# Two layers in one kernel: shared unit's last step behind the sorted steps, the last layer's gate product on GpSimd and its first tile begun in attention's last row

## The chip, the cores and the metric

One core of a Trainium2 chip runs the program, in one launch. The metric is the device time of one execution in microseconds, from the profile's start of the program to its end on that core. All times are medians of several executions where nothing else is said.

## What is computed

4096 tokens of 256 numbers (float32) go through two layers. Each has an attention part and a feed-forward part, both wrapped in the same way: layernorm, scale and shift from a conditioning vector, the part, a gate, and the addition to the tokens.

```python
h = _layernorm(x) * (1 + cb) + sb
x = x + gb * _L0_ffn_ref(h, ...)        # layer 0: two rounds of experts
h = _layernorm(x) * (1 + ca) + sa
x = x + ga * _L1_attn_ref(h, ...)       # layer 1: linear attention, 16 heads
h = _layernorm(x) * (1 + cb) + sb
x = x + gb * _L1_ffn_ref(h, ...)        # layer 1: 8 experts, top 2
```

The feed-forward part of layer 0 runs two rounds. In each, a token goes to 2 of 6 experts, chosen and weighted by a router, and also to 2 shared units, which see every token; their outputs and the token itself are added and normalised. The feed-forward part of layer 1 (stage D below) returns `x + experts(rms(x))`, with `x` being the modulated `h`: so the last layer's result is `x + gb*h + gb*experts(...)`. The term `gb*h` is "the gate product".

## The kernel before, in words

The instructions of each engine are written out by hand, engine by engine, with semaphores between them; an engine runs its own list in order. The stages are A (attention of layer 0), B (its two rounds of experts), C (attention of layer 1) and D (experts of layer 1). The tokens stay in SBUF as `b.x`, 8 tiles of 512 tokens (`NB = 8`), each of 4 chunks of 128.

**Stage B.** A round has 37 steps of 512 rows: 8 "new" (shared unit 0 on tile t), 8 "old" (shared unit 1 on tile t, whose product is joined to that of the new step, so that one down-projection does for both) and 21 "sort" steps (`NBB = 21`), each a block of 512 rows of one expert. `Round` (L1004) lists them. Every engine goes through iterations j = -1 to 36, and in iteration j it deals with up to three steps: `now` = j, `after` = j + 1, `third` = j + 2. TensorE (`b_tensor`, L1181) does:

```python
gate(after); turn(third); up(after); down(now)
```

where `turn` transposes the rows of a step. For a sort step it waits for the four indirect gathers that bring its rows (`r.gathered`). Weights are loaded raw by SyncE (`b_sync`, L1044, into four buffers `w_raw`), rounded by ScalarE and split into a low part by VectorE for each step that is `fresh`; shared units are so once a round. Between iterations 6 and 12 the routing goes on beside the steps; its last product is the index of the gathers, computed by VectorE in `index_vector` (L1698, L1704) at the end of iteration 12. GpSimd (`b_gpsimd`, L1709) then issues six blocks' gathers, and from then on four gathers and four scatters by turns; the gathers of the first four blocks wait for the transposes of the last old step, because all share the four buffers `got`, and scatters of a block wait for `r.o`, its output in `b.sent`, which VectorE writes in `send` (L1555). VectorE's order in an iteration is: low parts and transposed rows of `third`, product of `after` (for an old step also the addition of the shared product, L1539), output of `now`. When all scatters have landed, the next round, or stage C, fetches the rows back (`fetch_sync`, L1128; `close_sync`, L1779).

**Stage C** (`m_vector`, `m_tensor`, `m_scalar`, `m_gpsimd`) is a pipeline over the tiles; iterations j run from -3 to 9. At j = 8 VectorE divides tile 7 (`divide`) and adds the output of tile 6 to the tokens (`project`, L1988), at j = 9 that of tile 7. Each is there as soon as TensorE has it.

**Stage D's preparation** starts on every engine when the last tile is through (`rc.x`). Per tile: VectorE takes mean and variance (`stats`, L2116, L2120), GpSimd 1/sqrt (`rs`, L2168 and L2170, with a small op of the helper `absorb` at L178 ahead of it), VectorE modulates (`modulate`, two passes over four chunks, L2130 and L2134) into `p_h`, ScalarE sums squares, GpSimd takes 1/sqrt of that (`rs2`), TensorE transposes (L2231), ScalarE copies, TensorE multiplies by the router (L2236) and by a diagonal matrix of the gate (L2244, `p_diag`): that is the gate product, and VectorE adds it to the tokens from PSUM (`residual`, L2147). VectorE's order is modulate(t), stats(t+1), residual(t-1), logits(t-1). Behind tile 7's logits and residual the routing begins (`routed_vector`, L921).

## Time and profile before

| | us |
|---|---|
| three runs | 2035.42, 2036.41, 2038.35; median 2036.41 |
| the profiled execution | 2036.51 |
| its span, first to last instruction | 2034.6 |
| TensorE busy | 1766.5 (87%) |
| VectorE busy | 1402.5 (69%) |
| ScalarE busy | 1029.3 (51%) |
| GpSimd busy | 821.1 (40%) |
| mean granted TensorE clock | 0.927 of full speed |

A line of the timeline gives start and duration in us from the span's start, the engine (PE is TensorE, PEld its weight loads, DVE VectorE, ACT ScalarE, POOL GpSimd, SP SyncE), the line of the kernel, the operation, what it writes and reads, the shapes, how many were merged into the line, and in brackets how long the engine had been idle before and what released it. L167 is the line of a helper that makes every three-pass matmul of the experts. In busy times a DMA issued by GpSimd counts as its instruction. Shares of the whole span are averages over stages with different limits; the stretches that the change touches are read one by one below.

### The profile page before, as it was taken

The numbers are of one execution on the slowest core, as the hardware profiler recorded it, in microseconds if no ns is written. First come the engines' busy times: TensorE is split into PE (matmuls) and PEld (weight loads), VectorE is DVE, ScalarE is ACT, GpSimd is POOL, SyncE is SP. The second block draws the span as 40 slices with busy tenths as digits, with TensorE's granted clock in tenths as the row PEclk, the third lists the DMA queues.
The fourth block names the chain that finished last, engine by engine and source line by source line (L and its number), as shares of the span: only waits on it lengthen the run. The fifth ranks groups of instructions, "written<-read, shape, count | busy, mean of one in ns | idle before, by whom it ended". The sixth has DMA issues, their size and how long they took to land. (4 is left out here: it accounts for less than half of the span.)

```text
span 2034.6 us, 31786 instructions
## 1 busy us (share of the span) xinstructions
PE 1766.5 (87%) x11154; PEld 1559.6 (77%) x11154; DVE 1402.5 (69%) x2513; ACT 1029.3 (51%) x2078; POOL 821.1 (40%) x868
## 2 busy tenths in 40 slices
PE   5899999999978999999949999996499883899990
PEld 4788888888877878888838788886266683899990
DVE  4665556546433888777756987775798687688886
ACT  4344334434412344555546355553688353788882
POOL 2132232323211114777721157776221030788840
PEclk8899999999998899999969999998699966899995
DMA  4100000000023131666553226664600013688857
GB/s 155 62 1 11 10 10 0 10 10 0 10 88 103 55 105 40 202 192 202 168 190 122 91 78 199 203 186 146 221 32 1 1 63 114 206 278 277 257 193 258
DMA packets 146216, 231.43 MB, mean 114 GB/s; under 512 B 28082, under 2 KB 103092, under 8 KB 141108
## 3 DMA queue, kind: packets, MB, share of 16 engines
q1 hardware_dynamic: 122484, 165.47, 24.6%
q0 software_dynamic: 23616, 64.52, 10.5%
q8 instruction: 60, 0.98, 0.2%
q14 instruction: 56, 0.46, 0.1%
HBM read 174.07 MB, written 55.33 MB: 113 GB/s over the span
## 5 line engine op out<-in xcount | busy, mean ns | idle before, releaser
L178 POOL TENSOR_TENSOR spare_g<-neg_half 128x1 f32<-128x1 f32 x80 | 20.7, 259 | 622.2 <-ACT a_sg L538 142.5
L167 PE MATMUL bank<-gT_hi,w_hi 128*128 128x512 f32 x592 | 246.0, 416 | 2.4 <-DVE gT_lo L1526 2.4
L167 PE MATMUL bank<-gT_hi,w_lo 128*128 128x512 f32 x592 | 237.3, 401 | 0.0
L167 PE MATMUL bank<-gT_lo,w_hi 128*128 128x512 f32 x592 | 236.2, 399 | 0.0
L1731 POOL DMA_INDIRECT got<-b_rows,b_gather_i x168 | 171.9, 1023 | 65.1 <-issue 50.6
L1526 DVE TENSOR_TENSOR gT_lo<-bank,gT_hi 128x512 fp32r<-128x512 f32 x148 | 97.0, 689 | 132.4 <-ACT gT_hi L1334 99.1
L1364 ACT ACTIVATE m_hi<-gs 128x512 fp32r<-128x512 f32 x116 | 73.0, 633 | 128.3 <-DVE gs L1533 69.0
L167 PEld LDWEIGHTS bank<-gT_hi,w_lo 128*128 128x128 f32 x592 | 113.2, 191 | 27.6
L167 PE MATMUL bank<-w_hi,m_hi 128*128 128x256 f32 x464 | 130.5, 281 | 2.8 <-DVE shared L1555 1.4
L167 PEld LDWEIGHTS bank<-gT_hi,w_hi 128*128 128x128 f32 x592 | 113.6, 192 | 22.9 <-DVE gT_lo L1526 2.5
L167 PEld LDWEIGHTS bank<-gT_lo,w_hi 128*128 128x128 f32 x592 | 113.9, 192 | 21.5
L167 PE MATMUL bank<-w_lo,m_hi 128*128 128x256 f32 x464 | 130.4, 281 | 0.0
L167 PE MATMUL bank<-w_hi,m_lo 128*128 128x256 f32 x464 | 130.1, 280 | 0.0
L2390 POOL DMA_INDIRECT d_got<-d_rows,d_gather_i x78 | 95.7, 1227 | 68.8 <-DVE d_gather_i L2321 45.4
L2396 POOL DMA_INDIRECT d_kept<-d_sent,d_scatter_i x78 | 97.6, 1252 | 45.9 <-DVE d_sent L2551 24.6
L884 POOL TENSOR_TENSOR a_aTm<-a_aT,masks 128x512 f32<-128x512 f32 x56 | 71.4, 1286 | 107.2 <-PE bank L416 82.6
L1355 ACT ACTIVATE gs<-bank,w_cols 128x512 f32<-128x512 f32 x84 | 57.7, 690 | 97.3 <-PE bank L167 97.3
L1738 POOL DMA_INDIRECT b_kept<-sent,b_scatter_i x88 | 90.4, 1028 | 26.8 <-issue 26.8
L167 PE MATMUL bank<-d_gT_hi,v_hi 128*128 128x256 f32 x312 | 93.0, 298 | 1.8 <-DVE d_gT_lo L2531 1.8
L577 ACT ACTIVATE a_ax<-bank 128x512 f32<-128x512 f32 x48 | 28.7, 597 | 128.0 <-PE bank L416 128.0
L1334 ACT ACTIVATE gT_hi<-bank 128x512 fp32r<-128x512 f32 x148 | 82.0, 598 | 21.1 <-PE bank L1202 20.9
L167 PE MATMUL bank<-v_hi,d_m_hi 128*128 128x256 f32 x312 | 91.3, 293 | 1.4 <-issue 0.9
(455 smaller groups left out, 5731.2 us busy)
## 6 DMA issues: line engine op xcount, KB each, us to landing
v_raw<-in_units SPq DMA_DIRECT2D x39, 1024.0 KB, 5.0
w_raw<-in_units SPq DMA_DIRECT2D x52, 256.0 KB, 4.9
shared<-in_units SPq DMA_DIRECT2D x40, 256.0 KB, 4.4
b_rows<-x SPq DMA_DIRECT2D x16, 512.0 KB, 2.9
got<-b_rows SPq DMA_DIRECT2D x16, 512.0 KB, 3.9
close_back<-b_kept SPq DMA_DIRECT2D x16, 512.0 KB, 7.8
d_back<-d_kept SPq DMA_DIRECT2D x16, 512.0 KB, 8.5
w_raw<-b_folded SPq DMA_DIRECT2D x24, 256.0 KB
```

The source lines that it names most:

```text
L167: ins = pe.matmul(out, a, b, start=first and n == 0, stop=last and n == of - 1)
L178: eng.tensor_tensor(b.spare_g[:, i:i + 1], b.neg_half[:, 0:1], b.neg_half[:, 0:1], ALU.mult)
L577: act.activation(b.ax[:, :], B[1][:, :], ACT.Copy).then_inc(s.ax.sem, 1)
L884: g.tensor_tensor(four(b.aTm[l % 2][:, :]), four(b.aT[:, :]), mid(b.maskT[:, l, :], CT), ALU.mult).then_inc((s.aTm if l else s.aTm0).sem, 1)
L1334: act.activation(b.gT_hi[st.par][:, f, :], B[6 + f][:, :], ACT.Copy).then_inc(r.gT_hi.sem, 1)
L1355: act.activation(product_of(b, st)[:, o, :], B[2 + o][:, :], ACT.Silu, bias=b_bias(b, st, 1, o)).then_inc(r.sg.sem, 1)
L1364: act.activation(b.m_hi[st.par][:, o, :], b.gs[:, o, :], ACT.Copy).then_inc(r.m_hi.sem, 1)
L1526: v.tensor_tensor(b.gT_lo[st.par][:, f, :], B[6 + f][:, :], f32(b.gT_hi[st.par][:, f, :]), ALU.subtract).then_inc(r.gT_lo.sem, 1)
L1731: g.indirect_dma_start(b.got[:, kg % 4, c, :], None, dram.rows[rnd], bass.IndirectOffsetOnAxis(b.gather_i[:, q:q + 1], 0)).then_inc(r.gath ...
L1738: g.indirect_dma_start(dram.kept[rnd], bass.IndirectOffsetOnAxis(b.scatter_i[:, q:q + 1], 0), b.sent[kg % SENDS][:, c, :], None).then_inc( ...
L2390: g.indirect_dma_start(b.got[n % 6][:, c, :], None, rows, bass.IndirectOffsetOnAxis(b.gather_i[:, q:q + 1], 0)).then_inc(r.gathered[n % 6] ...
L2396: g.indirect_dma_start(kept, bass.IndirectOffsetOnAxis(b.scatter_i[:, q:q + 1], 0), b.sent[k % 4][:, c, :], None).then_inc(r.scattered[k % ...
```

## The change

Three things:

1. In stage B the old step of tile 7 goes behind the 21 sort steps (`LATE = 1`). Its unit's weights are loaded, rounded and split again (`LATE_LOAD`), its rows reloaded into a buffer of `got` that has come free; the gathers of the first blocks wait for the old step that is last now (tile 6). The order of the buffers of the next stage's fetches is turned, so that the late step's buffers are taken last, and two waits are put into SyncE's queue: before the third fetch of round 1, and before the constants of stage C. Stage C's buffers move within SBUF.
2. In stage C, at j = 8, VectorE does D's statistics of tiles 0 and 1 and D's modulation of tile 0. The waits for `rc.x` at the start of D fall away on VectorE, ScalarE and GpSimd, and on TensorE it stands behind the transposes of tile 0.
3. In D's preparation GpSimd multiplies the modulated tile by the gate, in two halves of 128x512 per tile, into a new buffer `p_gh`; the first half stands before 1/sqrt of the next tile, the second behind it. The 16 diagonal matmuls per tile and the two products that made the diagonal are gone. VectorE's residual is one addition of 128x1024 from SBUF.

```diff
+C_GAP = 5168
...
-STEPS, LB, WM = 2 * NB + NBB, 2 + NBB, KD * D
+LATE = 1
+FRONT_STEPS, LATE_LOAD = 2 * NB - LATE, 2 + NBB
+STEPS, LB, WM = 2 * NB + NBB, 3 + NBB, KD * D
...
-        order = [("new", t) for t in range(NB)] + [("old", t) for t in range(NB)] + [("sort", k) for k in range(NBB)]
+        order = [("new", t) for t in range(NB)] + [("old", t) for t in range(NB - LATE)]
+        order += [("sort", k) for k in range(NBB)] + [("old", t) for t in range(NB - LATE, NB)]
...
-            load = {"new": 0, "old": 1}.get(kind, 2 + n)
+            load = {"new": 0, "old": 1 if j < FRONT_STEPS else LATE_LOAD}.get(kind, 2 + n)
...
+
+
+def row_slot(t, rnd):
+
+    return t % 4 if t < NB - LATE else (rnd * NBB + NBB + t - (NB - LATE)) % 4
...
-    q0, t0, expert = rnd * LB, rnd * NB, {0: slice(0, 1), 1: slice(1, 2)}
+    q0, t0, expert = rnd * LB, rnd * NB, {0: slice(0, 1), 1: slice(1, 2), LATE_LOAD: slice(1, 2)}
...
-            sp.wait_ge(r.joined.sem, r.joined.at(rnd * NB + NB - 1))
-        if n >= 2:
+            sp.wait_ge(r.joined.sem, r.joined.at(rnd * NB + NB - LATE - 1))
+        if 2 <= n < LATE_LOAD:
...
         for t in range(BACKS):
+            if t == BACKS - 1:
+                sp.wait_ge(r.gT_ps.sem, r.gT_ps.at(STEPS - 1))
             fetch_sync(sp, b, r, dram.kept[0], t)
...
-    for t in range(NB):
+    for t in range(NB - LATE):
...
-            biases(n - 1)
+            if n - 1 < LATE_LOAD:
+                biases(n - 1)
+    for t in range(NB - LATE, NB):
+        sp.wait_ge(r.gT_ps.sem, r.gT_ps.at(first_sort(rnd * NBB + NBB - 4 + t - (NB - LATE))))
+        sp.dma_start(b.got[:, row_slot(t, rnd), :, :], rows_of(dram.rows[rnd], t)).then_inc(r.reloaded[t % 4].sem, 16)
...
-    return (kg // NBB) * STEPS + 2 * NB + kg % NBB
+    return (kg // NBB) * STEPS + FRONT_STEPS + kg % NBB
...
-    return (kg // NBB) * OUTS + NB + kg % NBB
+    return (kg // NBB) * OUTS + NB - LATE + kg % NBB
...
-            src = lambda c, f: b.got[:, t % 4, c, f * P:(f + 1) * P]
+            src = lambda c, f: b.got[:, row_slot(t, rnd), c, f * P:(f + 1) * P]
...
-    first, rounds = 2 * NB, (NBB - 2) // TURNS
+    first, rounds = FRONT_STEPS, (NBB - 2) // TURNS
...
-            act.wait_ge(done.sem, done.at(rnd * (OUTS if done is r.down_ps else STEPS) - 1))
+            ended = LATE if st.load % LB == 0 else 0
+            act.wait_ge(done.sem, done.at(rnd * (OUTS if done is r.down_ps else STEPS) - 1 - ended))
...
         if k >= 4:
...
         else:
-            g.wait_ge(r.gT_ps.sem, r.gT_ps.at(rnd * STEPS + 2 * NB - 1))
+            g.wait_ge(r.gT_ps.sem, r.gT_ps.at(rnd * STEPS + FRONT_STEPS - 1))
...
     old_rows(0)
+    sp.wait_ge(r.o.sem, r.o.at(2 * OUTS - 1))
     sp.dma_start(b.heads, d["consts"][:, 1, :]).then_inc(s.load_c_small.sem, 16)
...
+        if j == NB:
+            d_stats_vector(v, after, q, 0)
         if is_tile(j - 1):
             divide(j - 1)
+        if j == NB:
+            d_modulate_vector(v, after, q, 0)
         if is_tile(j - 2):
             project(j - 2)
+        if j == NB:
+            d_stats_vector(v, after, q, 1)
         if is_tile(j):
...
         if is_tile(j + FRONT - 2):
...
-    def stats(t):
...
-    def modulate(t):
...
+def d_stats_vector(v, b, r, t):
...
+def d_modulate_vector(v, b, r, t):
...
+        v.wait_ge(r.gh.sem, r.gh.at(t - 2))
...
-        for i in range(2):
-            v.wait_ge(r.gh.sem, r.gh.at(t, i + 1))
-            xt = b.x[:, (t * CT + 2 * i) * D:(t * CT + 2 * i + 2) * D]
-            v.tensor_tensor(xt, xt, b.bank[6 + i][:, :], ALU.add).then_inc(r.xh.sem, 1)
-
-    stats(0)
-    for k in range(KD):
-        v.tensor_tensor(b.p_diag[:, k, :], b.ident, b.mod[:, GB, k * P:(k + 1) * P], ALU.mult).then_inc(r.diag.sem, 1)
-    for t in range(NB):
-        modulate(t)
+        v.wait_ge(r.gh.sem, r.gh.at(t))
+        v.tensor_tensor(tile_of(b, t), tile_of(b, t), flat(b.p_gh[t % 2][:, :, :]), ALU.add).then_inc(r.xh.sem, 1)
+
+    for t in range(1, NB):
+        d_modulate_vector(v, b, r, t)
...
-            stats(t + 1)
-        if t >= 1:
-            residual(t - 1)
-            logits(t - 1)
+            d_stats_vector(v, b, r, t + 1)
+        residual(t - 1)
+        logits(t - 1)
...
+    def gated(t, i):
+        par = t % 2
+        g.wait_ge(r.h.sem, r.h.at(t, 2 * i + 2))
+        if t >= 2:
+            g.wait_ge(r.xh.sem, r.xh.at(t - 2))
+        g.tensor_tensor(b.p_gh[par][:, 2 * i:2 * i + 2, :], b.p_h[par][:, 2 * i:2 * i + 2, :], mid(b.mod[:, GB, :], 2), ALU.mult).then_inc(r.gh.sem, 1)
+
     rs(0)
     for t in range(NB):
+        gated(t, 0)
         if t + 1 < NB:
             rs(t + 1)
+        gated(t, 1)
         rs2(t)
...
         pe.wait_ge(r.hT.sem, r.hT.at(t))
+        if t == 0:
+            pe.wait_ge(m.x.sem, m.x.at(NB - 1))
...
-        if t >= 1:
-            pe.wait_ge(r.xh.sem, r.xh.at(t - 1))
-        for c in range(CT):
-            for k in range(KD):
-                at = (c % 2) * D + k * P
-                ins = pe.matmul(b.bank[6 + c // 2][:, at:at + P], b.p_hT[par][:, k, c * P:(c + 1) * P], b.p_diag[:, k, :], start=True, stop=True)
-            if c % 2:
-                ins.then_inc(r.gh.sem, 1)
...
-                b.back = [b.got[:, 2 * i:2 * i + 2, :, :] for i in range(2)] + [b.sent_both]
+                b.back = [b.sent_both, b.got[:, 2:4, :, :], b.got[:, 0:2, :, :]]
...
-            b.close_back, b.x_old = [sb(sc, f"close_back{t}", [P, PICKS, CT, D]) for t in range(CLOSE_BUFS)], [sb(sc, f"x_old{t}", [P, CT, D]) for t in range(CLOSE_BUFS)]
...
+            b.x_old = [sb(sc, f"x_old{t}", [P, CT, D]) for t in range(1, CLOSE_BUFS)]
+            b.c_gap = sb(sc, "c_gap", [P, C_GAP])
+            b.x_old.insert(0, sb(sc, "x_old0", [P, CT, D]))
+            b.close_back = [sb(sc, f"close_back{t}", [P, PICKS, CT, D]) for t in range(CLOSE_BUFS)]
...
-                b.p_h, b.p_xn, b.p_sq = ([sb(e, f"pd_{n}{i}", [P, CT, D]) for i in range(2)] for n in ("h", "xn", "sq"))
+                b.p_h, b.p_gh, b.p_xn, b.p_sq = ([sb(e, f"pd_{n}{i}", [P, CT, D]) for i in range(2)] for n in ("h", "gh", "xn", "sq"))
...
-                b.p_diag = sb(e, "pd_diag", [P, KD, P])
...
-            m_vector(v, bC, s, link, rb, rp, rc)
+            m_vector(v, bC, s, link, rb, rp, rc, bD, rd)
...
-                       rs2=("wu_lo", 1), hn=("weighed", CT), gh=("mixed", 2), xh=("added", 2), hT_ps=("hT", KD), hT=("folded", KD), logit_ps=("logit_ps", 1), logits=("logits", 1),
+                       rs2=("wu_lo", 1), hn=("weighed", CT), gh=("mixed", 2), xh=("added", 1), hT_ps=("hT", KD), hT=("folded", KD), logit_ps=("logit_ps", 1), logits=("logits", 1),
...
-        rd.router, rd.diag = signal("d_router", KD), signal("d_diag", KD)
...
-            g.wait_ge(rc.x.sem, rc.x.at(last))
...
-            act.wait_ge(rc.x.sem, rc.x.at(last))
...
-            pe.wait_ge(rc.x.sem, rc.x.at(last))
-            d_prep_tensor(pe, bD, rd)
+            d_prep_tensor(pe, bD, rd, rc)
...
```

## Rows read from the trace of the kernel before

**Rows 1.** The page: its first line.
```profile
span 2034.6 us, 31786 instructions
```

**Rows 2.** Instruction groups of GpSimd, 804 to 1029: busy us, mean ns | idle before.
```profile
L1731 POOL DMA_INDIRECT got<-b_rows,b_gather_i x84 | 86.5, 1030 | 32.6 <-issue 25.3 <-PE bank L1202 7.3
```

**Rows 3.** Timeline of GpSimd: start us, us, instruction [idle before <-releaser].
```profile
804.70 1.22 POOL L1731 DMA_INDIRECT got<-b_rows,b_gather_i  x1 [7.30 <-PE bank L1202]
...
1023.60 0.97 POOL L1738 DMA_INDIRECT b_kept<-sent,b_scatter_i  x1 [0.30 <-issue]
...
1413.06 0.97 POOL L1738 DMA_INDIRECT b_kept<-sent,b_scatter_i  x1 [0.30 <-issue]
```

**Rows 4.** Timeline of VectorE in the token steps.
```profile
803.25 0.20 DVE L1704 TENSOR_SCALAR b_gather_i<-b_gather_i 128x84 int32<-128x84 int32 x1
...
1014.71 1.28 DVE L1555 TENSOR_TENSOR shared<-bank,w_b 128x512 f32<-128x512 f32 x2
...
1019.26 0.69 DVE L1555 TENSOR_TENSOR sent<-bank,w_b 128x512 f32<-128x512 f32 x1 [0.66 <-PE bank L167]
...
1409.99 0.69 DVE L1555 TENSOR_TENSOR sent<-bank,w_b 128x512 f32<-128x512 f32 x1 [0.66 <-PE bank L167]
```

**Rows 5.** Timeline of VectorE, last layer's preparation.
```profile
1622.66 0.69 DVE L1988 TENSOR_TENSOR x<-x,bank 128x512 f32<-128x512 f32 x1 [1.27 <-PE bank L2058]
...
1633.67 1.67 DVE L2130 SCALAR_TENSOR_TENSOR pd_h<-x,p_mv,mod 128x256 f32<-128x256 f32 x4 [1.66 <-POOL p_rs L2170]
...
1638.58 0.68 DVE L2147 TENSOR_TENSOR x<-x,bank 128x512 f32<-128x512 f32 x1
...
1677.11 1.66 DVE L2130 SCALAR_TENSOR_TENSOR pd_h<-x,p_mv,mod 128x256 f32<-128x256 f32 x4
...
1689.54 0.28 DVE L921 COPY r_z<-logits 128x256 f32<-128x256 f32 x1
```

**Rows 6.** Instruction groups of VectorE, 1633.6 to 1677, columns as in rows 2.
```profile
L2147 DVE TENSOR_TENSOR x<-x,bank 128x512 f32<-128x512 f32 x12 | 8.1, 678 | 5.8 <-PE bank L2244 5.8
```

**Rows 7.** Timeline of TensorE in round 0.
```profile
802.71 1.09 PE L1202 MATMUL bank<-ident,got 128*128 128x128 f32 x8
...
812.56 1.04 PE L1202 MATMUL bank<-ident,got 128*128 128x128 f32 x8
...
999.67 1.03 PE L1202 MATMUL bank<-ident,got 128*128 128x128 f32 x8
```

**Rows 8.** Line 1731 by itself, its last line.
```profile
DMA to landing us min/median/max: 2.7/3.3/6.8
```

**Rows 9.** Timeline of TensorE after a long stop.
```profile
1734.55 1.97 PE L2434 MATMUL bank<-ident,d_got 128*128 128x128 f32 x8 [8.60 <-DMA d_got<-d_rows,d_gather_i]
```

**Rows 10.** Stretches, line 167: us, busy (count) of TensorE, weight loads, clock, DMA.
```profile
1734.00:1741.00 7.00, 3.50 (x16) 3.50 (x17) 0.50 0.38 97
```

**Rows 11.** Timeline of GpSimd in four places.
```profile
52.11 1.27 POOL L884 TENSOR_TENSOR a_aTm<-a_aT,masks 128x512 f32<-128x512 f32 x1 [3.99 <-PE bank L416]
...
1067.83 1.16 POOL L178 TENSOR_TENSOR spare_g<-neg_half 128x1 f32<-128x1 f32 x1 [10.90 <-ACT got L1428]
...
1439.23 1.13 POOL L1900 TENSOR_TENSOR p_rs<-p_rs,neg_half 128x4 f32<-128x4 f32 x1
...
1632.63 1.01 POOL L2170 TENSOR_TENSOR p_rs<-p_rs,neg_half 128x4 f32<-128x4 f32 x1
```

**Rows 12.** Timeline of VectorE in three of these places.
```profile
52.08 1.58 DVE L670 SCALAR_TENSOR_TENSOR a_h_next<-a_h_next,a_rs,mod 128x256 f32<-128x256 f32 x1
...
1067.71 1.23 DVE L1437 TENSOR_TENSOR x<-x,got 128x1024 f32<-128x1024 f32 x1
...
1438.25 1.64 DVE L1435 SCALAR_TENSOR_TENSOR close_back<-close_back,r_gb 128x256 f32<-128x256 f32 x4
```

**Rows 13.** Timeline of TensorE, first tile of the preparation.
```profile
1630.43 1.94 PE L2231 MATMUL bank<-ident,pd_h 128*128 128x128 f32 x8 [7.80 <-DVE pd_h L2134]
1633.06 3.58 PE L2236 MATMUL bank<-router_D,pd_hT 128*128 128x8 f32 x16 [0.69 <-ACT pd_hT L2200]
```

44 lines of the change are left out of this document (21 added, 23 removed).

## The prediction, made blind

> **What bounds the kernel now.** The edits touch three stretches, so I read the chain of waits first (in both rounds it runs through GpSimd's issues), then one timeline for each engine of each stretch. The execution read took 2036.51 us around a span of 2034.6 [rows 1]; the median of three runs is 2036.41, the same for this purpose. What can be told from no change is about 0.2%, or 4.1 us.
>
> *Token steps, both rounds.* The reader is to see that GpSimd, not TensorE, ends a round. In round 0 its 84 gathers and 84 scatters (44 and 40, by their two kinds of source) run from 804.70 to 1028.4; the only wait for another engine is the 7.3 us before the first gather, all else is issue gaps of 0.30 [rows 2]. VectorE has the last block's rows ready at 1019.95 (1019.26 + 0.69), but GpSimd starts their scatters only at 1023.60: 3.65 us of queue. In round 1 it is 1410.68 against 1413.06, 2.4 us [rows 3, 4]. The next stage starts from the last scatter.
>
> *Preparation of the last layer.* From the last residual of attention (1622.66 + 0.69 = 1623.35) to the start of routing (1689.54) go 66 us; from one tile's modulation to the next it takes (1677.11 - 1633.67)/6 = 7.24 us, of which VectorE waits about 1 us per tile for TensorE's gate product (5.8 us in six tiles) [rows 5, 6].
>
> **Edit 1: last shared-unit step moved behind the 21 sorted steps.** TensorE's order inside an iteration is gate(next), transposes(next but one), up(next), down(now). The first sorted block's transposes now stand where the last "old" step's stood: at 802.71 instead of 812.56 [rows 7]. They need four gathers. Those no longer wait for the old step's transposes (done 803.80, first gather 0.9 later) but for the index, finished at 803.45 [rows 3, 4, 7]. So the first gather starts at about 804.35, only 0.35 earlier. The fourth starts 3 x 1.33 (1.03 and the gap of 0.30 [rows 2]) = 4.0 later and lands 3.0 after that (the gathers of this line land 2.7 us after issue at the least, 3.3 in the median [rows 8]): 811.35. **TensorE stands for 8.7 us**, and the first block starts 1.2 us earlier than before instead of 9.85.
>
> Then the clock. After a stop of 8.60 us, TensorE comes back at 1734.55, and the granted clock is 0.50 (1.2 GHz, the lower of its two levels) up to 1741.0, 6.5 us on [rows 9, 10]. Half of 6.5 us is 3.2; TensorE has a little less than that to lose, as part of such a stretch is issue, and I take 3.0. Bounds: half of it (1.5) to half as much again (4.5).
>
> At the other end the sorted block is now followed by an old step. A sorted step takes (999.67 - 812.56)/20 = 9.36 us [rows 7]. Before, the last block's rows came 3.96 us after the last but one's (1019.95 - 1015.99 [rows 4]), as nothing stood in between. Now they come like those of a block in the middle, a full 9.36 after, and 1.3 later still, because VectorE adds the old step's shared product first (two more 128x512 passes, which cost what the two of the row at 1014.71 cost). Sum for round 0: -1.2 + 3.0 + (9.36 + 1.3 - 3.96) = +8.5, so the rows are ready at 1028.45, and the scatter starts 0.9 later: 1029.35 against 1023.60, **+5.75**. Round 1 has the same pattern with 1.25 us less queue: **+7.0**. GpSimd now waits for VectorE in front of the last four scatters in each round.
>
> The rest of edit 1 costs nothing as long as its cover stands. The shared unit is loaded again (768 KB) and rounded again: ScalarE and VectorE do for it what they do for every sorted block, in a place where before the last sorted block stood. On SyncE's queue its loads come after the biases of the last block but two, and the reload of the tile's rows comes last of all; SyncE has a whole step for it before TensorE wants it, and if that cover went, the late step alone would be later, and the last scatter with it since down(now) stands behind gate and up of the late step. The late step's own output ends some 5 us after the last block's, while scatters are issued and land. Two waits are added on SyncE's queue. Behind the one before the third fetch stand the stores and fetches of round 1, behind the one before the small constants stand attention's seven constant loads and the fetches of tiles 1 to 7; both end with the late step, while the first two fetches (or the three loads of tile 0) are still under way. The new order of buffers moves no work.
>
> **Edit 2: first tile begun in attention's last row of work.** VectorE's statistics of tile 0 fall into its idle time before the last division, its modulation before the last-but-one residual, statistics of tile 1 before the last one. VectorE waits there for TensorE anyway and the last residual keeps its 1623.35. Modulation of tile 1 begins then, against 1633.67 before [rows 5]: **-10.3**. The two diagonal products (0.5) are in it.
>
> **Edit 3: gate product by GpSimd.** Removed: 16 matmuls per tile and the wait for them. Added: two products of 128x512 on GpSimd per tile, priced by its nearest row, 1.27 us for the same shape with two SBUF inputs and one of them repeated [rows 11]. GpSimd's total per tile is 2.5 + 3.0 = 5.6 us, so it does not become the bound by its work. But the two engines get in each other's way:
> - At 52.08 VectorE starts a 128x256 op with two SBUF inputs 0.03 before GpSimd's product starts, and takes 1.58 us. Ops of this size take 0.40 to 0.48 undisturbed (four of them 1.64, at 1438.25), so **+1.10**: it stands until GpSimd is through [rows 11, 12]. Both halves of the new product meet such ops: the first is released by chunk 2 of the modulated tile, while VectorE writes chunk 3 and 4; the second is queued behind 1/sqrt of the next tile, which is just what VectorE's next modulation waits for. Two such stops per tile: 2.2.
> - The other way round, GpSimd's small op at 1067.83 takes 1.16 us instead of 0.19, to the end of VectorE's 128x1024 addition of two SBUF tiles that began at 1067.71 [rows 11, 12]. The residual becomes exactly this form (before, one input came from PSUM), and it starts right when GpSimd is to compute the next 1/sqrt. So its 1.22 lies in front of the 1.5 of that (VectorE's next modulation starts at 1633.67, 1.5 to 1.7 after its statistics end, the row of 1632.63 being its last part [rows 11]).
>
> Per tile: modulation and statistics 4.91 (1633.67 to 1638.58) + stops 2.2 + residual 1.22 + 1/sqrt 1.5 = **9.8 us in place of 7.24**. First interval 8.7 (no second half queued yet), five more of 9.8: tile 7 begins at 1623.35 + 8.7 + 49.0 = 1681.05, 3.9 later than 1677.11. Behind it: modulation 3.2 with two stops 2.1, transposes to logits at the low clock 6.2 (1630.43 to 1636.64 [rows 13]), logits and residual 1.5: 1694.1 against 1689.54, **+4.6** for edits 2 and 3 together. Bounds: +2.2 with the high clock at the end; +8.2 if a product takes 1.5.
>
> A rule weighed. While GpSimd computes 1/sqrt of four columns for 1.13 us at 1439.23, VectorE's four ops with two SBUF inputs, begun at 1438.25, go on at their usual pace (1.64) [rows 11, 12]; I give these small ops no price. The Trainium skill, page "SBUF — State Buffer", section "Who interferes with whom", has it that whichever of the two starts first holds the pair for its whole instruction and the other blocks fully. By that rule the second 1/sqrt of each tile would stop VectorE too; what it would give is a rival below.
>
> **Sum.** 2036.5 + 5.75 + 7.0 + 4.6 = 2053.85, say **2054**, 0.9% slower.
>
> **Rivals.**
> 1. *The product runs beside VectorE for nothing.* Place: the two stops and the late 1/sqrt per tile. Then a tile takes 4.91 + 1.5 + 0.1 = 6.5, tile 7 begins at 1662.4 and routing at 1673.3 (3.2 + 6.2 + 1.5 behind it): -16.2 in place of +4.6, so 2033, faster than before by 3; with the high clock at the end 2031. It decides where the tile falls under 7.24 + 10.3/6 = 8.9 us: below, the preparation gains. For it: GpSimd's work has room. Against it: [rows 11, 12], both ways. Chance 0.09.
> 2. *The late step costs nothing at the scatters* (GpSimd's queue still hides the last block; no stop of 8.7 us, or one that is made up). Then 2036.5 - 0.7 + 4.6 = 2040.4. For it: GpSimd has 2.4 to 3.65 us of queue. Against it: TensorE has no idle time between sorted steps to make anything up in. Chance 0.06.
> 3. *Both*: 2036.5 - 0.7 - 16.2 = 2019.6. Chance 0.04.
> 4. *Every GpSimd op stops VectorE*, the second 1/sqrt of each of seven tiles as well, 1.0 each: 2061. Against it: the last pair of [rows 11, 12]. This is the rule of the Trainium skill's page "SBUF — State Buffer" taken to the letter. Chance 0.05.
> 5. The forecast, 0.76.
>
> **Numbers.** The forecast's own range: edit 1 9.5 to 15.5 (clock 1.5 to 4.5 per round), edits 2 and 3 +2.2 to +8.2, not all at one end: 2047 to 2061. Down to rival 2 and up over rival 4: **2040 to 2062**, which leaves out rivals 1 and 3 and a little more. Faster by over 0.2% (under 2032.3): rival 3 and half of rival 1, 0.08. Within 0.2%: the rest of rival 1 and half of rival 2, 0.08. Slower: 0.84.
>
> **What would show it.** Right: in each round TensorE idle some 8 us before the first sorted block's transposes, released by a gather, then matmuls at half clock; GpSimd waiting for VectorE's output before the last four scatters; that scatter some 6 us later relative to the round's start; the new product at about 1.3 us, modulation ops of 1.5 us among those of 0.48, the small op in front of 1/sqrt at about 1.2 us, tiles 9.8 us apart. Wrong: tiles 6.5 us apart (edit 3), or the last scatter still preceded by an issue gap of 0.30 alone (edit 1).

## The result and the profile after

The changed kernel takes 2047.39 us (median of six executions, 2045.98 to 2053.41), the kernel before in the same session 2037.87 (2035.42 to 2044.20). The ratio is 1.0048, with a 95% interval from 1.0031 to 1.0065: slower by 0.5%, some 9.8 us. The prediction said slower, by 17.5 us. The signs and places were right; nearly every term was too large.

To see where the time went I cut both traces at the same marks. "Round" is from its first transposes to the start of the last block's four scatters, "seam" from there to the next round's first transposes, "attention" from the second round's mark to the end of the last residual, "preparation" from there to the start of routing.

| stretch | before | after | difference | forecast |
|---|---|---|---|---|
| start to first transposes of the token steps | 658.04 | 660.43 | +2.39 | 0 |
| round 0 | 365.56 | 369.00 | +3.44 | +5.75 |
| seam | 21.42 | 22.17 | +0.75 | 0 |
| round 1 | 368.04 | 371.04 | +3.00 | +7.0 |
| attention | 210.29 | 209.88 | -0.41 | 0 |
| preparation | 66.19 | 69.41 | +3.22 | +4.6 |
| rest of the last layer | 345.07 | 345.50 | +0.43 | 0 |
| span | 2034.61 | 2047.43 | +12.82 | +17.35 |

The first row is not the change's: among the 14 profiled kernels of this study, with the same work up to there, that mark stands at 657.9 to 658.6 in seven and at 659.9 to 660.5 in the other seven, kernels with and without the late step on either side; the kernel before happened to be among the early ones. What is left, 10.4, is close to the ratio.

The page's first line, against [rows 1]:

```profile
span 2047.4 us, 31578 instructions
```

**The token steps.** Instruction groups of GpSimd from 805 to 1035 us (columns as in [rows 2]):

```profile
L1747 POOL DMA_INDIRECT got<-b_rows,b_gather_i x84 | 85.3, 1015 | 31.6 <-issue 25.3 <-DVE b_gather_i L1720 6.3
L1754 POOL DMA_INDIRECT b_kept<-sent,b_scatter_i x44 | 45.0, 1024 | 17.9 <-issue 13.1 <-DVE sent L1571 4.8
```

The gathers now wait for the index and no longer for TensorE, and before the scatters there is a wait for VectorE's output that did not exist. The timeline of GpSimd puts it in front of the last block, in both rounds (against [rows 3]):

```profile
806.13 1.56 POOL L1747 DMA_INDIRECT got<-b_rows,b_gather_i  x1 [6.35 <-DVE b_gather_i L1720]
...
1029.43 0.97 POOL L1754 DMA_INDIRECT b_kept<-sent,b_scatter_i  x1 [4.84 <-DVE sent L1571]
...
1422.64 0.96 POOL L1754 DMA_INDIRECT b_kept<-sent,b_scatter_i  x1 [4.51 <-DVE sent L1571]
```

The timeline of VectorE shows what GpSimd waits for, the output of the last sorted block, in one line for its two halves (against [rows 4]); and the late step's own output, 4.8 us later, for which the trace shows nobody waiting:

```profile
1027.87 1.28 DVE L1571 TENSOR_TENSOR sent<-bank,w_b 128x512 f32<-128x512 f32 x2
1032.70 0.69 DVE L1569 TENSOR_TENSOR x<-x,bank 128x512 f32<-128x512 f32 x1 [3.55 <-PE bank L1261]
```

The timeline of TensorE (against [rows 7]): transposes of the old step in front, of the first, second and last sorted block and of the late step. The stop of 8.33 names no releaser; the first block's fourth gather starts at 810.49, so it is by this time, 2.8 us, that I take it for the landing. Between the first two sorted blocks stand 11.7 us, not 9.8 as before, and the matmuls inside begin 0.43 us apart up to 817.2 and 0.23 after it.

```profile
793.74 1.09 PE L1217 MATMUL bank<-ident,got 128*128 128x128 f32 x8 [0.16 <-DVE b_found L1710]
...
813.31 1.94 PE L1217 MATMUL bank<-ident,got 128*128 128x128 f32 x8 [8.33 <-issue]
...
825.01 1.04 PE L1217 MATMUL bank<-ident,got 128*128 128x128 f32 x8
...
1002.32 0.93 PE L1217 MATMUL bank<-ident,got 128*128 128x128 f32 x7
...
1011.63 0.60 PE L1217 MATMUL bank<-ident,got 128*128 128x128 f32 x4
```

Two stretches behind that stop (columns as in [rows 10], here all lines: us, busy of TensorE, weight loads, VectorE, ScalarE, GpSimd, granted clock, DMA):

```profile
813.00:815.00 2.00, 1.69 (x9) 1.72 (x9) 0.00 (x0) 0.57 (x1) 1.69 (x2) 0.50 0.41 109
815.00:820.00 5.00, 5.00 (x24) 4.21 (x23) 3.55 (x6) 1.14 (x3) 3.78 (x5) 0.76 0.31 90
```

**The preparation.** Timeline of VectorE and GpSimd, end of the last residual and one whole tile (against [rows 5, 11]):

```profile
1631.83 0.69 DVE L2005 TENSOR_TENSOR x<-x,bank 128x512 f32<-128x512 f32 x1 [1.27 <-PE bank L2081]
1632.43 1.67 DVE L2154 SCALAR_TENSOR_TENSOR pd_h<-x,p_mv,mod 128x256 f32<-128x256 f32 x4
...
1650.44 1.26 POOL L2206 TENSOR_TENSOR pd_gh<-pd_h,mod 128x512 f32<-128x512 f32 x1
...
1650.61 2.57 DVE L2154 SCALAR_TENSOR_TENSOR pd_h<-x,p_mv,mod 128x256 f32<-128x256 f32 x4 [1.43 <-POOL p_rs L2189]
...
1652.52 1.12 POOL L2199 TENSOR_TENSOR p_rs<-p_rs,neg_half 128x4 f32<-128x4 f32 x1
...
1653.10 2.67 DVE L2157 SCALAR_TENSOR_TENSOR pd_h<-pd_h,p_rs,mod 128x256 f32<-128x256 f32 x4
...
1654.05 1.44 POOL L2206 TENSOR_TENSOR pd_gh<-pd_h,mod 128x512 f32<-128x512 f32 x1 [0.40 <-DVE pd_h L2157]
...
1657.42 1.19 DVE L2170 TENSOR_TENSOR x<-x,pd_gh 128x1024 f32<-128x1024 f32 x1
...
1657.58 1.08 POOL L181 TENSOR_TENSOR spare_g<-neg_half 128x1 f32<-128x1 f32 x1 [2.09 <-DVE p_mv L2142]
...
1659.01 1.01 POOL L2189 TENSOR_TENSOR p_rs<-p_rs,neg_half 128x4 f32<-128x4 f32 x1
```

Each pass of four takes 2.6 us beside a product in place of 1.67 alone: two stops per tile. Ahead of the first pass VectorE waits 1.43 us. The second 1/sqrt (1652.52) lies beside both passes, and the sum of 2.57 + 2.67 has room for the two stops and nothing else: it stops nobody. From 1632.43 one interval of 8.64 and five of 9.54 lead to tile 7 at 1688.76; routing begins at 1701.93.

### The profile page after: what moved, and what is told of

It is laid out like the page before. It is cut to its first block and busy times, and to the rows that moved or that the text cites. A ratio compares the mean times of both kernels' runs of the same rounds, so it can differ in the third digit from the quotient of the medians.

```text
span 2047.4 us, 31578 instructions
## 1 busy us (share of the span) xinstructions
PE 1759.2 (86%) x11026; PEld 1552.0 (76%) x11026; DVE 1418.9 (69%) x2509; ACT 1031.0 (50%) x2084; POOL 850.4 (42%) x884
## 3 DMA queue, kind: packets, MB, share of 16 engines
q0 software_dynamic: 23616, 64.52, 10.3%
## 5 line engine op out<-in xcount | busy, mean ns | idle before, releaser
L181 POOL TENSOR_TENSOR spare_g<-neg_half 128x1 f32<-128x1 f32 x80 | 27.0, 338 | 591.3 <-ACT a_sg L541 142.3
L1380 ACT ACTIVATE m_hi<-gs 128x512 fp32r<-128x512 f32 x116 | 72.9, 633 | 128.9 <-DVE gs L1549 67.5
L170 PEld LDWEIGHTS bank<-w_hi,m_hi 128*128 128x128 f32 x464 | 88.0, 190 | 8.0 <-issue 5.5
L1754 POOL DMA_INDIRECT b_kept<-shared,b_scatter_i x80 | 82.8, 1035 | 25.3 <-issue 24.1
```

The lines of the kernel that those rows point to most:

```text
L170: ins = pe.matmul(out, a, b, start=first and n == 0, stop=last and n == of - 1)
L181: eng.tensor_tensor(b.spare_g[:, i:i + 1], b.neg_half[:, 0:1], b.neg_half[:, 0:1], ALU.mult)
L1380: act.activation(b.m_hi[st.par][:, o, :], b.gs[:, o, :], ACT.Copy).then_inc(r.m_hi.sem, 1)
L1754: g.indirect_dma_start(dram.kept[rnd], bass.IndirectOffsetOnAxis(b.scatter_i[:, q:q + 1], 0), b.sent[kg % SENDS][:, c, :], None).then_inc( ...
```

## The experiments

All kernels were timed against the kernel before on the same chip and in the same session, where its median was 2037.9 to 2042.1; the expectations count from the 2036.4 that stand above, so the ratio is what to compare. The stretches are those of the table above; "steps" is round 0, seam and round 1 together.

| kernel | ratio [95%] | steps | attention | preparation | rest |
|---|---|---|---|---|---|
| before | 1 | 755.02 | 210.3 | 66.19 | 345.1 |
| changed | 1.0048 [1.0031, 1.0065] | 762.20 | 209.9 | 69.41 | 345.5 |
| late_only | 1.0037 [1.0024, 1.0050] | 761.83 | 209.4 | 67.54 | 346.6 |
| prep_only | 1.0007 [0.9999, 1.0016] | 754.86 | 213.7 | 69.47 | 345.0 |
| first_only | 0.9921 [0.9908, 0.9934] | 754.78 | 209.8 | 52.69 | 344.9 |
| late_down_first | 1.0011 [1.0002, 1.0021] | 754.20 | 213.3 | 67.75 | 346.4 |
| late_early_index | 0.9988 [0.9978, 0.9999] | 749.53 | 212.3 | 67.71 | 346.5 |
| late_both | 0.9969 [0.9959, 0.9979] | 745.75 | 212.4 | 68.34 | 346.0 |
| prep_no_product | 0.9950 [0.9935, 0.9965] | 755.15 | 210.1 | 56.98 | 345.7 |
| prep_resid_first | 1.0017 [1.0008, 1.0026] | 754.49 | 209.9 | 70.92 | 345.8 |
| prep_rs_between | 0.9933 [0.9916, 0.9950] | 754.50 | 209.9 | 56.07 | 344.8 |
| combo | 0.9904 [0.9887, 0.9920] | 742.67 | 211.5 | 53.99 | 346.8 |
| combo_tuned | 0.9895 [0.9878, 0.9911] | 745.26 | 212.3 | 53.27 | 345.6 |
| after_repaired | 0.9890 [0.9869, 0.9912] | 744.86 | 212.8 | 56.06 | 344.6 |

Attention's length is one thing to know before reading on: 209.4 to 213.7 us, without order in the edits (prep_only and prep_rs_between have the same token steps and the same attention, and differ by 3.8). A single profile is therefore good for a stretch, not for a total; totals are compared by the ratios.

**late_only: edit 1 by itself.** The functions of the last layer and of attention are those of before; against the changed kernel:

```diff
-            m_vector(v, bC, s, link, rb, rp, rc, bD, rd)
+            m_vector(v, bC, s, link, rb, rp, rc)
...
-            d_prep_tensor(pe, bD, rd, rc)
+            pe.wait_ge(rc.x.sem, rc.x.at(last))
+            d_prep_tensor(pe, bD, rd)
...
```

> Edit 1 alone (with its buffers and the two waits on SyncE's queue), the last layer's preparation as before. By the steps of the prediction, with the sizes that the two traces show (the row of sorted blocks begins 1.6 us earlier against the step in front of it, the low clock costs 1.9, the last rows come 6.55 later behind their block, 3.4 us of GpSimd's queue are used up): +3.5 in round 0, about +4 in round 1, so +7.5: 2044. Rival: the changed kernel is also 2.4 us late before its token steps begin; if the moved buffers or the added waits do that, this kernel shows it too and stands at +10, 2046.5. Rival: the late step costs nothing at the scatters, 2036.

Measured 1.0037, some 7.6 us, as the first theory had it; with prep_only's 1.0007 it makes 1.0044, inside the changed kernel's interval. Its rounds are the changed kernel's (369.0 and 371.4). In its profile the token steps are 6.8 longer than before; the preparation and the rest are 1.3 and 1.6 longer too, with the same work (see the last section), so the agreement of 7.6 with 7.5 is partly chance. Its seam is 21.44, as before: the 0.75 of the changed kernel's seam is left without a cause.

**prep_only: edits 2 and 3 by themselves.** The moved buffers and the two added waits of edit 1 stay in.

```diff
-LATE = 1
+LATE = 0
-STEPS, LB, WM = 2 * NB + NBB, 3 + NBB, KD * D
+STEPS, LB, WM = 2 * NB + NBB, 2 + LATE + NBB, KD * D
```

> Edits 2 and 3 alone (the late step is off, LATE = 0). By the steps with measured sizes: tile 1 is modulated 10.3 us earlier, six tiles take 9.5 instead of 7.24, and the tail 1 to 2 more: +3.4, so 2040. The product counts with two stops of VectorE of 1.0 each per tile, the late small op with 1.0. Rival: edits 2 and 3 lengthen the rest of the last layer as well (routing starts 12.5 later in the changed kernel, the end is 12.8 later), +5 or more.

The preparation takes 69.47, the 3.3 more that were expected; the rest of the layer is unchanged, so the rival falls. The ratio's upper end, 1.0016, is just these 3.3 us; by the ratio alone this kernel can't be told from the kernel before. Its rounds are those of before (365.5 and 367.9), so the moved buffers and the added waits cost nothing there.

**first_only: edit 2 by itself.** In d_prep_vector, d_prep_gpsimd and d_prep_tensor the gate product is the diagonal one of before.

```diff
-        gated(t, 0)
         if t + 1 < NB:
             rs(t + 1)
-        gated(t, 1)
```

> Edit 2 alone: the first tile is begun in attention's last row, the gate product stays with TensorE and its diagonal. If the early start is worth what the prediction gave it, tile 1 is modulated at the end of the last residual (plus 0.5 for the diagonal) and the tiles stay 7.24 apart: -9.5, so 2027. Rival: TensorE, which cannot start tile 0's transposes before attention's last product, becomes the bound for the first tiles and takes the gain back: -3 to -5, 2032. Rival: nothing gained, 2036.

All three theories were too cautious: 0.9921, 16 us faster, and the preparation is 13.5 shorter. From the last residual's end to tile 1 it is 0.3 (1625.04 to 1625.36) in place of 10.3, as expected; but the tiles also stand only 6.75 apart, not 7.24. Timeline of this kernel, VectorE and TensorE:

```profile
1643.76 1.28 DVE L2171 TENSOR_TENSOR x<-x,bank 128x512 f32<-128x512 f32 x2
...
1645.60 1.67 DVE L2153 SCALAR_TENSOR_TENSOR pd_h<-x,p_mv,mod 128x256 f32<-128x256 f32 x4 [0.46 <-POOL p_rs L2192]
...
1652.02 1.95 PE L2259 MATMUL bank<-router_D,pd_hT 128*128 128x8 f32 x16 [1.38 <-ACT pd_hT L2222]
```

The two residual additions are one line without a wait between them, where before the second waited 1 us per tile for the product [rows 6]. With tile 0 begun early, TensorE's product of a tile is there when VectorE comes to it; the loop is VectorE's own work and 0.46 of waiting. Measured from this kernel, edit 3 costs 69.4 - 52.7 = 16.7 us, not the few that stand between the changed kernel and the kernel before. Of these, 1.3 lie behind tile 7, where TensorE's clock differs as well. Stretches from tile 7 to routing, changed kernel and first_only (columns as above):

```profile
1688.76:1701.93 13.17, 7.91 (x36) 7.32 (x35) 7.63 (x12) 6.08 (x18) 7.86 (x9) 0.50 0.25 87
...
1665.84:1677.73 11.89, 10.18 (x72) 9.75 (x72) 6.21 (x14) 6.25 (x19) 2.99 (x6) 0.86 0.36 122
```

The granted clock is 0.50 (1.2 GHz) there in all six kernels without the gate product on TensorE, prep_no_product among them, and 0.70 to 0.86 in the eight that have it; in the kernel before it is 0.86. The clock is not what the 1.3 us are, though: prep_no_product (below), at 0.50 and without the two stops of 1.9, takes 11.3 for this stretch, so what the lower clock costs there, the missing matmuls save.

**late_down_first: the end of a round.** In the iteration of the last sorted block, on TensorE and on VectorE:

```diff
+        ahead_of_late = j == FRONT_STEPS + NBB - 1
+        if ahead_of_late:
+            down(now)
         if after is not None:
             gate(after)
...
-        if now is not None and now.out is not None:
+        if now is not None and now.out is not None and not ahead_of_late:
             down(now)
...
+        ahead_of_late = j == FRONT_STEPS + NBB - 1
+        if ahead_of_late:
+            send(now)
         if after is not None:
             gated(after)
...
```

> Edit 1 alone, but in the iteration in which the last sorted block is finished, TensorE does its down-projection ahead of the late step's gate and up, and VectorE writes its output ahead of the late step's product. If the loss at the end of a round is the 9.36 + 1.3 - 3.96 us by which the last block's rows come later (measured 6.55), they come 4 us after the block before again, GpSimd's own queue hides them, and the last scatter starts about 1 us earlier than in the kernel before (with the first gather): -3.5 to -4.5 per round against the late step alone, so 2035 to 2037. Rival: the end of a round hangs on the late step's own output or on its reload: no change against the late step alone, 2044.

Measured 1.0011: 5.3 us of late_only's 7.6 are gone (7 to 9 were expected). In the profile the token steps are 7.6 shorter than late_only's and 0.8 shorter than before; what keeps the ratio above 1 lies behind them (preparation and rest are 1.6 and 1.3 longer than before, last section). Timeline of this kernel, end of round 0 (SPq is SyncE's DMA queue):

```profile
1022.58 0.69 DVE L1574 TENSOR_TENSOR sent<-bank,w_b 128x512 f32<-128x512 f32 x1 [0.65 <-PE bank L170]
...
1024.72 0.97 POOL L1760 DMA_INDIRECT b_kept<-sent,b_scatter_i  x1 [0.30 <-issue]
...
1031.52 0.68 DVE L1529 TENSOR_TENSOR w_lo<-w_raw,w_hi 128x512 fp32r<-128x512 f32 x1
1032.23 0.33 SPq L1077 DMA_DIRECT2D w_raw<-in_units  x1
1032.74 0.93 SPq L1147 DMA_DIRECT2D sent<-b_kept  x2
```

In front of the last scatters there is again nothing but the issue gap, and round 0 takes 364.5, 4.5 less than with the late step alone and 1.1 less than before. But the seam grows from 21.4 to 23.8. The fetches (1032.74) stand on SyncE's queue behind a load of the next round's weights, which waits for VectorE's low part of the late step (that is one of two limits here; combo_tuned below takes it away, and the seam stays as long). So the cover that the prediction gave to the late step's extra work holds only as long as the last scatters are late themselves.

**late_early_index: the start of a round.**

```diff
-ROUTE_AT, COUNT_AT, INVERT_AT, GATES_AT = NB - 2, NB - 1, NB + 1, NB + 5
+ROUTE_AT, COUNT_AT, INVERT_AT, GATES_AT = NB - 2, NB - 1, NB, NB + 5
...
         if j == COUNT_AT + 1:
             places_vector(v, b, link, r)
+            hot_vector(v, b, r, rnd, 0)
...
-        if j == COUNT_AT + 1:
-            hot_vector(v, b, r, rnd, 0)
```

ScalarE's first quarter of the same work goes behind the weights of its iteration.

> Edit 1 alone, with the routing's inversion begun one iteration earlier (iterations 8 to 11 instead of 9 to 12), so that the index of the gathers is ready about 11 us before TensorE reaches the first sorted block. Its first quarter must be built inside iteration 8, where VectorE takes 3.8 us more ahead of the product and TensorE waits for it: some 4 to 5 us lost there. If TensorE's 8 us without rows and the low clock behind them (1.9 by the sorted blocks' own interval) are what spoils the late step's start, they are gone: 10 gained, 4 to 5 lost, -5 to -6 per round against the late step alone, 2033 to 2036. Rival: gathers that start 11 us earlier only move the wait (GpSimd, at 1.3 us per issue, or the reload), and nothing is gained: 2045 or more.

Measured 0.9988, 10 us less than late_only, 5 per round (6.1 and 6.3 by the profiles). Timelines of this kernel, GpSimd's first gather and TensorE's first sorted block:

```profile
799.21 1.22 POOL L1748 DMA_INDIRECT got<-b_rows,b_gather_i  x1 [7.77 <-PE bank L1217]
...
807.07 0.49 PE L1217 MATMUL bank<-ident,got 128*128 128x128 f32 x3
```

The gathers wait for the old step's transposes again, and TensorE comes to the first block without a stop, 9.8 us behind the transposes of the step in front (797.28) instead of 19.6. The 20 intervals of the sorted blocks are back at 187.1 us, as before, where late_only has 189.0 and 188.7: the 1.9 and 1.6 were the stop's. The price stands before it: from the first step's transposes to the fifteenth's it is 138.9 us, 5.6 more than before. 9.8 + 1.9 - 5.6 is the 6.1 of round 0. The last scatters still wait for VectorE (4.49 us at 1021.28).

**late_both: start and end.** Both diffs together.

> Edit 1 with the earlier index and with the last sorted block's down-projection ahead of the late step's gate. If the two losses add, it stands at -5 to -6 per round for the start and, as GpSimd's queue runs ahead now and no longer hides anything, up to -5 per round for the end: 2023 to 2030. What can take it back: SyncE's queue, where the fetches of the next stage stand behind the next round's first weights, which wait for VectorE's low part of the late step (seen in the kernel with the down-projection first: fetches 1.8 us later than the landing of the scatters allows).

Measured 0.9969, which is 2030 from the 2036.4 of the first runs: the upper end of the range. Round 0 takes 360.0 (5.5 less than before), round 1 361.7 (6.3 less), and the seam 24.05 takes 2.6 back. With these two moves the late step gains: edit 1 was not wrong in itself. Neither move was tried without the late step; there the gathers wait for the last old step, and the index is ready 0.35 us earlier than that (803.45 against 803.80 [rows 4, 7]), so I would expect little of the first.

**prep_no_product: what the two products cost.** This kernel leaves the gate out, so it computes another result; it is prep_only with the two products shrunk to 128x1 and one more wait.

```diff
+        v.wait_ge(r.xh.sem, r.xh.at(t - 2))
...
-        v.tensor_tensor(tile_of(b, t), tile_of(b, t), flat(b.p_gh[t % 2][:, :, :]), ALU.add).then_inc(r.xh.sem, 1)
+        v.tensor_tensor(tile_of(b, t), tile_of(b, t), flat(b.p_h[t % 2][:, :, :]), ALU.add).then_inc(r.xh.sem, 1)
...
-        g.tensor_tensor(b.p_gh[par][:, 2 * i:2 * i + 2, :], b.p_h[par][:, 2 * i:2 * i + 2, :], mid(b.mod[:, GB, :], 2), ALU.mult).then_inc(r.gh.sem, 1)
+        g.tensor_tensor(b.p_gh[par][:, 2 * i, 0:1], b.p_h[par][:, 2 * i, 0:1], b.mod[:, GB, 0:1], ALU.mult).then_inc(r.gh.sem, 1)
```

> Edits 2 and 3 alone, with GpSimd's two products of 128x512 per tile shrunk to 128x1 (this leaves out the gate: the residual adds the ungated tile). Everything else stays. If the two products cost what VectorE's two stops of 1.0 and 1.1 show, a tile takes 7.5 instead of 9.54 us: modulation and statistics 4.9, small op held back by the residual 1.1, 1/sqrt 1.4; the preparation is 14 shorter, 2027. Rival: the interval is set by the chain residual, small op, 1/sqrt alone and stays above 9.

Tiles 7.63 apart (tile 2 to tile 7: 1631.17 to 1669.33), so the two products cost 9.54 - 7.63 = 1.91 per tile, which is the two stops. The ratio is 0.9950 where prep_only has 1.0007, the preparation 12.5 us shorter (14 were expected). Timeline of this kernel, VectorE and GpSimd:

```profile
1658.97 1.19 DVE L2171 TENSOR_TENSOR x<-x,pd_h 128x1024 f32<-128x1024 f32 x1
...
1659.13 1.08 POOL L181 TENSOR_TENSOR spare_g<-neg_half 128x1 f32<-128x1 f32 x1 [2.16 <-DVE p_mv L2142]
...
1661.69 1.67 DVE L2155 SCALAR_TENSOR_TENSOR pd_h<-x,p_mv,mod 128x256 f32<-128x256 f32 x4 [1.43 <-POOL p_rs L2190]
```

Both passes are back at 1.67; the held small op and the 1.43 of waiting are still there.

**prep_resid_first: the small op set free.**

```diff
         d_modulate_vector(v, b, r, t)
+        residual(t - 1)
         if t + 1 < NB:
             d_stats_vector(v, b, r, t + 1)
-        residual(t - 1)
         logits(t - 1)
```

> Edits 2 and 3 alone, with the residual ahead of the next tile's statistics instead of behind them. GpSimd's small op in front of 1/sqrt then meets no addition of two SBUF inputs. If it is the residual that holds it back (1.08 instead of 0.19 in each tile), the interval falls by 0.9 to 8.65 and the preparation by 5 to 6: 2035. Rival: the small op is late for another reason (it waits for the statistics in any case), no change: 2041.

The small op does take 0.19 now, and it is of no use: 1.0017, tiles 9.79 apart, 0.25 more than with the hold-back. The same view of this kernel:

```profile
1669.29 0.19 POOL L181 TENSOR_TENSOR spare_g<-neg_half 128x1 f32<-128x1 f32 x1 [3.23 <-DVE p_mv L2142]
...
1669.83 1.01 POOL L2189 TENSOR_TENSOR p_rs<-p_rs,neg_half 128x4 f32<-128x4 f32 x1
...
1670.97 2.58 DVE L2154 SCALAR_TENSOR_TENSOR pd_h<-x,p_mv,mod 128x256 f32<-128x256 f32 x4 [1.68 <-POOL p_rs L2189]
```

VectorE pays the residual's 1.2 us in either place, and then waits for all of 1/sqrt (1.68). My expectation took the delay of an engine's op for a cost of the loop without asking what the other engine does in that time.

**prep_rs_between: 1/sqrt hidden.** In d_modulate_vector:

```diff
-    v.wait_ge(r.rs.sem, r.rs.at(t))
+    v.wait_ge(r.mv.sem, r.mv.at(t))
...
+    v.wait_ge(r.rs.sem, r.rs.at(t))
     for c in range(CT):
         v.wait_ge(r.xn.sem, r.xn.at(t, c + 1))
```

> Edits 2 and 3 alone, with VectorE's wait for 1/sqrt between the two passes of the modulation. If small op and 1/sqrt behind the residual (1.4 us of VectorE's waiting per tile) are the other half of edit 3's price, the first pass hides them: a tile takes 8.1 us (9.54 - 1.43), with the two stops still there, and the whole 8 to 9 less than edits 2 and 3 alone. Rival: GpSimd's queue (both products, two 1/sqrt, small ops, 5.6 us and more where they are held back by the first pass) moves behind and its second product or 1/sqrt becomes what VectorE waits for: 9 us per tile, 3 less.

Better than either theory: tiles 7.30 apart, the preparation 56.07, ratio 0.9933. With GpSimd's product in place, edits 2 and 3 now gain 14 us against before. The same view of this kernel:

```profile
1648.34 1.39 DVE L2138 BATCH_NORM_STATS2 p_stats<-x 128x6 f32<-128x256 f32 x4
...
1648.86 1.27 POOL L2207 TENSOR_TENSOR pd_gh<-pd_h,mod 128x512 f32<-128x512 f32 x1
...
1651.27 1.66 DVE L2154 SCALAR_TENSOR_TENSOR pd_h<-x,p_mv,mod 128x256 f32<-128x256 f32 x4
...
1651.88 1.13 POOL L2190 TENSOR_TENSOR p_rs<-p_rs,neg_half 128x4 f32<-128x4 f32 x1
1652.98 1.26 POOL L2207 TENSOR_TENSOR pd_gh<-pd_h,mod 128x512 f32<-128x512 f32 x1
...
1653.05 2.67 DVE L2158 SCALAR_TENSOR_TENSOR pd_h<-pd_h,p_rs,mod 128x256 f32<-128x256 f32 x4
```

Two things went away: the wait of 1.43 (the first pass starts right behind the logits, and 1/sqrt lies beside it), and one of the two stops, which was not the aim. GpSimd's order has shifted by half a tile, so one of its products falls under VectorE's statistics, whose four ops take 1.39 as ever. 1.43 + 0.9 is the 2.24 by which the tile is shorter, nearly. Against first_only, which leaves the product on TensorE, the preparation is still 3.4 us longer: edit 3 is made cheap, not made to pay.

**combo, combo_tuned and after_repaired: what the change could have given.** combo has the late step with both moves, and edit 2 with the gate product on TensorE. combo_tuned adds the moved wait for 1/sqrt and, on SyncE's queue in round 1:

```diff
         first_mats(n)
-        last_mat(n)
+        if rnd == 0 or n == 0:
+            last_mat(n)
...
             fetch_sync(sp, b, r, dram.kept[0], t)
+        last_mat(1)
```

> Edit 2 alone in the last layer (gate product by TensorE) together with edit 1 in its repaired form (index one iteration earlier, last sorted block's down-projection first). The two stretches have nothing in common, so if they add: -15.6 (edit 2 alone, ratio 0.9921) and -6.3 (repaired edit 1, ratio 0.9969), -22 against before, ratio 0.989. Rival: the late step's end collides with attention's first work or attention's clock gives part of it back: ratio 0.991 or more.

> The kernel of the two repaired edits with two more changes. First, VectorE's wait for 1/sqrt stands between the two passes of the modulation instead of ahead of both: VectorE waited 0.46 to 0.49 per tile there, so tiles 6.3 us apart instead of 6.72 if VectorE is the bound, -3; rival: TensorE becomes the bound (it waits about 1 us per tile for ScalarE's copies), -1 or nothing. Second, SyncE's last load of the next round's second unit stands behind the fetches instead of ahead of them: it waits for VectorE's low part of the late step and held the fetches back by 1 to 2 us, so the next round starts 1 to 2 us earlier; rival: VectorE's late low parts hold the round back anyway, nothing. Together -2 to -5 against the kernel without them.

combo is at 0.9904 where 0.989 was expected, inside its interval, which also holds the rival's 0.991. combo_tuned can't be told from it. Its tiles are 6.2 to 6.5 apart and one 7.6, a mean of 6.46 against combo's 6.75, and the preparation is 0.7 shorter. Its seam is 23.84 against 23.55: no gain, though the fetches come earlier. Timeline of this kernel:

```profile
1026.21 0.93 SPq L1149 DMA_DIRECT2D sent<-b_kept  x2
...
1033.62 1.29 DVE L1533 TENSOR_TENSOR w_lo<-w_raw,w_hi 128x512 fp32r<-128x512 f32 x2
1034.82 1.67 DVE L1458 SCALAR_TENSOR_TENSOR sent<-sent,r_gb 128x256 f32<-128x256 f32 x4
```

The first fetch now starts 1.5 us behind the end of the last scatter's instruction (2.9 in late_both), and then the first use of its rows stands on VectorE behind the next round's low weight parts: the rival of the expectation. That first use comes 10.1 us behind the last scatter here and 7.4 in the kernel before and the changed kernel.

after_repaired is the changed kernel itself, GpSimd's product included, with three moves: INVERT_AT, the last sorted block's down-projection and output, and the wait between the passes.

> The changed kernel with all three edits, GpSimd's product included, and three moves: the routing's inversion one iteration earlier, the last sorted block's down-projection and output ahead of the late step's work, VectorE's wait for 1/sqrt between the two passes of the modulation. If the losses found one by one are all there is, the ratios multiply: 0.9969 (late step repaired) x 0.9933 (edits 2 and 3 with the wait moved) = 0.990, 20 below before and 29 below the changed kernel, as fast as the kernel with the gate product on TensorE. Rival: the losses of the changed kernel lie partly where the edits meet (its seam between the rounds was 0.75 longer than with the late step alone), and it stays at 0.995 or above.

Measured 0.9890: 2018.86 us against 2042.06 of the kernel before in that session. By ratios it is 0.9890/1.0048, 1.6% faster than the changed kernel, from three moves and no work saved. The product of the two repaired ratios, 0.990, lies inside its interval (0.9869 to 0.9912) and the rival's 0.995 outside: to some 4 us either way, the losses found one by one are all there is. It can't be told from combo_tuned (0.9895), which has the gate product on TensorE; by the stretch, 56.06 against 53.27, TensorE is still the better place.

## Why the prediction was right in sign and too large

**First block of a round (-1.2).** Right in kind, measured -1.6 and -1.7 (19.57 and 19.46 us behind the transposes of tile 6's old step, against 21.19 and 21.20). The stop was 8.33 where 8.7 was forecast; the first gather came 0.9 earlier against that step, not 0.35. late_early_index shows that this stop, with the clock behind it, is what makes the late step's start useless.

**The clock (+3.0).** Mis-sized: +1.9 and +1.4, by the 20 intervals from the first to the last sorted block (189.0 and 188.5 against 187.1). late_early_index, without the stop, has 187.1 in both rounds, so it is the stop's price. I carried 6.5 us at the low clock over from a stop of 8.60 [rows 9, 10]; here the matmuls were back at full speed 3.9 us after the stop of 8.33 in round 0, and 2.9 after one of 8.24 in round 1. It lay inside the bounds of 1.5 to 4.5 in round 0 and just below in round 1.

**Last block's rows behind their transposes (+6.7).** Measured +6.55 in both rounds (26.83 against 20.28); late_down_first took it away and GpSimd's wait with it. This was the best term of the sum.

**Rows to scatter (0.9) and the queue.** GpSimd starts 0.28 after VectorE's output, not 0.9. With -1.6 + 1.9 + 6.55 = 6.8, less 3.65 of queue, plus 0.28, round 0 gives 3.46, as the table has it. In round 1 it is -1.7 + 1.4 + 6.55 - 2.4 + 0.3 = 4.1, and 1.1 more is missing: first to fifteenth transposes take 136.0 in place of 137.1. The kernels without the late step have 136.5 to 137.1 there, so perhaps 0.8 of it is the late step's; how stays open.

**Edit 2 (-10.3).** Right, and incomplete. Tile 1 begins 0.1 us before the end of the last residual's line, as forecast. What I missed is that the same head start also takes away VectorE's wait for TensorE in every tile. With it, edit 2 alone is worth 13.5 and not 10.3.

**Edit 3 (9.8 us per tile).** Measured 9.54. The stops: 2.2 forecast, 1.91 measured. "Residual 1.22" was right as a number and wrong as a reason: it is VectorE's own work, not GpSimd's late small op (prep_resid_first). "1/sqrt 1.5": 1.43. The end behind tile 7 took 13.2 (13.0 forecast, with the low clock that the profile then shows). Together +3.2 in place of +4.6, the difference being five intervals of 0.26. What the forecast had not priced is the other side: with the early start in place, the same product on TensorE needs 6.75 per tile and 11.9 at the end (first_only). The rival's rule, that the preparation gains below 8.9 us per tile, holds: at 7.30 it gives 6 x 1.6 = 9.6, measured 10.1.

**Rivals.** Of "the product runs beside VectorE for nothing" the profile shows the opposite; but one of the two products can be put beside the statistics, where it is free. "The late step costs nothing at the scatters" fell with the waits of 4.84 and 4.51. "Every GpSimd op stops VectorE" fell too: the 1/sqrt ops of 1.0 to 1.1 us lie beside passes of 1.66. The Trainium skill, page "SBUF — State Buffer", section "Who interferes with whom", says that a VectorE instruction with two SBUF inputs contends with a GpSimd instruction that reads SBUF, and the passes of 2.57 and 2.67 beside a product bear that out. It says there too that a VectorE instruction with at most one SBUF input does not contend, outside the two-port modes, and the statistics at 1.39 beside a product agree. The rule that whoever starts first holds the pair for the whole instruction stands on the same page, section "SBUF: two separate sides"; a 128x4 op of 1.13 us does not do that here (1651.88 beside the pass of 1.66 at 1651.27).

The whole error is in sizes, 17.35 against 9.7 in the three stretches: 2.3 in round 0 (clock 1.1, gap 0.6, first block 0.4, last block's rows 0.15), 4.0 in round 1 (clock 1.6, gap 0.6, first block 0.5, last block's rows 0.15, the 1.1 above), 1.4 in the preparation. All of them lie on the same side.

## What to carry to other kernels

Work that is moved off the end of a stage uncovers what it used to hide at the start: here the index of the gathers, which had to come one iteration earlier for the move to gain anything. Where an engine's last product is what the next stage waits for, the moved work must also come behind it on every engine, not only in the list of steps. When an op is delayed by another engine, ask what its waiting reader does meanwhile before pricing the delay; and before moving an op to another engine, measure the form without the move, since the wait that it was to remove may go with the other edit (first_only).

## What was not expected of the hardware

- After a stop of 8.33 us TensorE was granted 0.50 (1.2 GHz) up to 817.2, 3.9 us, and after one of 8.24 in round 1 for 2.9 us, where a stop of 8.60 in the kernel before was followed by 6.5 us of it.
- The product stops VectorE where VectorE's op starts 0.03 us ahead of it (52.08 [rows 11, 12]) and where it starts 0.07 to 0.17 us behind (1650.61, 1653.05); a product of 1.26 us lengthens one pass by 0.9 to 1.0 us.
- Four statistics ops take 1.39 us beside a product, and the product 1.27 beside them: no loss on either side.
- Four kernels with the late step and the old preparation have a preparation of 67.5 to 68.3 and a rest of 346.0 to 346.6, where the kernel before has 66.2 and 345.1, though these stretches do the same work. The preparation's part lies behind tile 7: up to there they take what the kernel before takes, from there to routing 13.7 to 14.6 us in place of 12.4, at a granted clock of 0.70 to 0.76 in place of 0.86. Why the late step should change the clock there stays open, and so does the rest.
- The 16 gate matmuls per tile go with a clock of 0.71 from tile 1 to tile 7 in the kernel before and 0.83 in first_only; the changed kernel, without them, has 0.54 there and 0.50 from tile 7 on.
